# Mamba-2 mixer step: decays, readouts and Gram products issued sooner, squares summed on VectorE, softplus in fewer operations

## The reference

```
zxbcdt = x @ W_in                         # gate, xBC (x, B, C), dt
xBC = silu(depthwise_conv4(xBC))
dt = softplus(dt + dt_bias);  A = -exp(A_log);  dA = exp(dt * A)
h = h * dA[t] + (dt[t] * x[t]) outer B[t];   y[t] = h . C[t]     # scan over 1024 tokens, 16 heads
y = (y + D_skip * x) * silu(gate)
y = y * rsqrt(mean(y*y) + eps) * norm_w
out = y @ W_out
```

## Time and profile before

| | |
|---|---|
| median of 3 runs | 1135.15 us |
| the profiled execution | 1135.18 us |
| its span, first to last instruction | 1133.1 us |
| TensorE busy | 1071.9 us (95%) |
| VectorE busy | 749.0 us (66%) |
| ScalarE busy | 574.2 us (51%) |
| GpSimd busy | 319.3 us (28%) |

### The profile page before, as it was taken

How to read it: one execution, slowest core, us unless ns; L and a number is a source line. 1 busy time by engine, 2 the same in 40 slices (tenths; PEclk the granted TensorE clock), 3 DMA queues, 4 the chain that set the end, 5 groups by cost and what they waited for, 6 DMA issues and landing times.

```text
span 1133.1 us, 18155 instructions
## 1 busy us (share of the span) xinstructions
PE 1071.9 (95%) x6912; PEld 934.0 (82%) x6912; DVE 749.0 (66%) x1311; ACT 574.2 (51%) x1190; POOL 319.3 (28%) x433
## 2 busy tenths in 40 slices
PE   6889999999999997889999999899999999999997
PEld 6778888888888885788998998887888888888886
DVE  6899999999999998657766687765432133223213
ACT  6856767676767673645665556563212311321220
POOL 1012223130313214343434444313312321321331
PEclk9899999999999999989999999999999999999999
DMA  5504031322313056501011101408012002002001
GB/s 197 199 3 147 31 116 47 101 60 87 108 39 127 2 201 196 194 2 29 11 38 38 38 1 38 140 19 282 15 38 75 1 19 93 1 1 75 1 1 56
DMA packets 41590, 81.22 MB, mean 72 GB/s; under 512 B 7456, under 2 KB 13472, under 8 KB 39456
## 3 DMA queue, kind: packets, MB, share of 16 engines
q1 hardware_dynamic: 41504, 80.06, 21.2%
HBM read 67.19 MB, written 12.85 MB: 71 GB/s over the span
## 4 chain that ended last, share of the span: by engine, by line
PE 60%; DVE 24%; ACT 7%; issue 5%; POOL 2%; DMA 1%; DVEq 0%; SPq 0%; POOLq 0%; ACTq 0%
PE banks L1853 20%; PE banks L801 12%; PE banks L1866 10%; PE banks L1502 8%; DVE a_L L658 4%; DVE a_xs L575 3%; PE banks L1472 3%; PE banks L931 2%; DVE c_gx L1366 1%; DVE c_cv L1342 1%; PE banks L923 1%; DVE a_L L672 1%; ACT c_a L1243 1%; DVE a_ygl L701 1%; PE banks L881 1%
## 5 line engine op out<-in xcount | busy, mean ns | idle before, releaser
L1753 ACT ACTIVATE d_sg<-banks,d_gs 128x512 f32<-128x512 f32 x64 | 44.0, 688 | 224.8 <-PE banks L1853 224.8
L1796 DVE SCALAR_TENSOR_TENSOR d_h<-banks,d_us,d_sg 128x512 f32<-128x512 f32 x64 | 48.1, 751 | 163.6 <-PE banks L1853 151.3
L1727 POOL TENSOR_TENSOR d_hl<-d_h,d_hh 128x512 fp32r<-128x512 f32 x64 | 83.2, 1300 | 158.3 <-ACT d_hh L1757 158.2
L575 DVE SCALAR_TENSOR_TENSOR a_xs<-a_xpre,a_cvec,a_xs 128x256 f32<-128x256 f32 x192 | 100.3, 537 | 6.4 <-ACT a_xs L446 1.8
L1866 PE MATMUL banks<-d_wd,d_hh 128*128 128x512 f32 x256 | 101.1, 395 | 0.0
L1866 PE MATMUL banks<-d_wd,d_hl 128*128 128x512 f32 x256 | 100.9, 394 | 0.0
L331 POOL TENSOR_TENSOR a_sg<-a_sg 128x512 f32<-128x512 f32 x16 | 24.5, 1533 | 221.8 <-ACT a_sg L438 221.8
L658 DVE TENSOR_TENSOR_SCAN a_L<-a_L,a_ident 128x512 f32<-128x512 f32 x64 | 78.4, 1225 | 2.2
L801 PE MATMUL banks<-a_xth,a_wxh 128*128 128x256 f32 x256 | 75.7, 296 | 0.4 <-DVE a_wxl L566 0.4
L462 ACT ACTIVATE a_xdt<-banks,a_dt 128x64 f32<-128x64 f32 x256 | 56.5, 349 | 36.4 <-PE banks L881 36.4
L801 PE MATMUL banks<-a_xth,a_wgh 128*128 128x256 f32 x256 | 74.9, 293 | 0.0
(11 more groups left out here) (285 smaller groups left out, 3144.6 us busy)
## 6 DMA issues: line engine op xcount, KB each, us to landing
a_L<-decays SPq DMA_DIRECT2D x16, 1024.0 KB, 5.1
a_xf<-in_x SPq DMA_DIRECT2D x16, 256.0 KB, 2.9
a_xr<-in_x SPq DMA_DIRECT2D x16, 256.0 KB, 2.7
tokens<-a_xr SPq DMA_DIRECT2D x16, 256.0 KB, 4.0
c_xb<-tokens SPq DMA_DIRECT2D x16, 256.0 KB, 3.2
d_xin<-tokens SPq DMA_DIRECT2D x16, 256.0 KB, 5.0
d_r<-tokens SPq DMA_DIRECT2D x16, 256.0 KB, 2.7
d_wd_codes<-in_down_w SPq DMA_DIRECT2D x4, 1024.0 KB, 9.1
```

What stands on the lines that cost most here:

```text
L575: ins = dve.scalar_tensor_tensor(out=dst, in0=src[:, k:k + T], scalar=vec[:, k:k + 1], in1=dst, op0=ALU.mult, op1=ALU.add)
L1727: pool.tensor_tensor(hl[:, m, :], h32[:, m % 2, :], hh[:, m, :].bitcast(F32), ALU.subtract).then_inc(s_hl, 1)
L1753: act.activation(sg[:, m % 2, :], ps_g[:, m % 2, :], ACT.Silu, scale=gs[:, m:m + 1]).then_inc(s_sg, 1)
L1796: dve.scalar_tensor_tensor(out=h32[:, m % 2, :], in0=ps_u[:, m % 2, :], scalar=us[:, m:m + 1], in1=sg[:, m % 2, :], op0=ALU.mult, op1=ALU. ...
```

## The change

Line numbers below are those of the kernel before for the old code. Five things change:

- ScalarE does `decay` and `bc_out` ahead of `high_y(2s-1)` and `square(2s-1)`, and `gram` ahead of `evict(s, 3)`.
- TensorE does `gram` between the two channel blocks of `x_proj(s, 3)`, `turn_z` in the middle of the first channel block of `x_proj(s, 0)`, and the second `sum_sq` behind `out_proj(2s-1)`.
- The additions of squares go from GpSimd to VectorE, the first two of the three; the third is left out, and `sum_sq` takes the last two blocks in two accumulating matmuls.
- `soft` has one operation, a reciprocal and a product in its second part in place of the flag, and one operation in its third part in place of five.
- VectorE's `low(2s-1)`, `mean_sq` and the additions have new places among the `conv_m`.

```diff
@@ gpsimd
-        def tree(n):
-            pool.wait_ge(s_sq, n + 1)
-            order(pool.tensor_tensor(sq[:, 0:4], sq[:, 0:4], sq[:, 4:8], ALU.add))
-            order(pool.tensor_tensor(sq[:, 0:2], sq[:, 0:2], sq[:, 2:4], ALU.add))
-            pool.tensor_tensor(sq[:, 0], sq[:, 0], sq[:, 1], ALU.add).then_inc(s_tree, 1)
...
-                tree(C * s - 2)
-                tree(C * s - 1)
                 scale(C * s - 2)
+                norm(C * s - 2)
                 scale(C * s - 1)
-                norm(C * s - 2)
@@ scalar
             evict(s, 2)
+            decay(s)
+            bc_out(s)
             if s:
                 high_y(C * s - 1)
                 square(C * s - 1)
-            decay(s)
-            bc_out(s)
+            gram(s)
             evict(s, 3)
-            gram(s)
@@ vector
                 dve.tensor_scalar(u, e, 1.0, None, ALU.add).then_inc(s_dt, 1)
                 dve.wait_ge(s_dt, 2 * s + 2)
-                order(dve.tensor_scalar(one, u, 1.0, None, ALU.is_equal))
+                order(dve.tensor_scalar(r, u, -1.0, SMALLEST, ALU.add, ALU.max))
+                order(dve.reciprocal(r, r))
+                order(dve.tensor_tensor(r, e, r, ALU.mult))
             else:
                 dve.wait_ge(s_ln, s + 1)
-                order(dve.scalar_tensor_tensor(out=u, in0=u, scalar=-1.0, in1=one, op0=ALU.add, op1=ALU.add))
-                order(dve.reciprocal(u, u))
-                order(dve.tensor_tensor(l, l, u, ALU.mult))
-                order(dve.tensor_tensor(l, l, one, ALU.add))
-                order(dve.tensor_tensor(l, l, e, ALU.mult))
+                order(dve.scalar_tensor_tensor(out=l, in0=l, scalar=SMALLEST, in1=r, op0=ALU.max, op1=ALU.mult))
...
+        def tree(n):
+            dve.wait_ge(s_sq, n + 1)
+            order(dve.tensor_tensor(sq[:, 0:4], sq[:, 0:4], sq[:, 4:8], ALU.add))
+            dve.tensor_tensor(sq[:, 0:2], sq[:, 0:2], sq[:, 2:4], ALU.add).then_inc(s_tree, 1)
...
+        tree(C * NS - 2)
         low(C * NS - 1)
+        tree(C * NS - 1)
@@ tensor
-            pe.matmul(ps_y[:, j, 0, 0:1], sg[:, 0, cols(j)], ones, start=True, stop=True).then_inc(s_sp, 1)
+            pe.matmul(ps_y[:, j, 0, 0:1], sg[:, 0, cols(j)], ones, start=True, stop=False)
+            pe.matmul(ps_y[:, j, 0, 0:1], sg[:, 1, cols(j)], ones, start=False, stop=True).then_inc(s_sp, 1)
...
+                part(0, KD // 2)
+                if m == 0:
+                    turn_z(s)
+                last = part(KD // 2, KD)
+                if m == 2 * p and p == 3:
+                    gram(s)
```

More of the change, by code:

```diff
@@ L108, in mamba2 @@
     LIMIT = 80.0
+    SMALLEST = 2.0 ** -24
     Z0 = 64
@@ L162, in mamba2 @@
     btok = sb("a_btok", [P, C, N], F32)
-    z, e, u, l, one, dt, a = (sb("a_" + n, [P, C, H], F32) for n in ("z", "e", "u", "l", "one", "dt", "a"))
+    z, e, u, l, r, dt, a = (sb("a_" + n, [P, C, H], F32) for n in ("z", "e", "u", "l", "r", "dt", "a"))
     e16 = sb("a_e16", [H, T], F32)
@@ L325, in gpsimd @@
         pool.wait_ge(s_const, 15 + HQ)
-        def tree(n):
-            j = n % C
-            sq = sg[:, :, cols(j)]
-            pool.wait_ge(s_sq, n + 1)
-            order(pool.tensor_tensor(sq[:, 0:4], sq[:, 0:4], sq[:, 4:8], ALU.add))
-            order(pool.tensor_tensor(sq[:, 0:2], sq[:, 0:2], sq[:, 2:4], ALU.add))
-            pool.tensor_tensor(sq[:, 0], sq[:, 0], sq[:, 1], ALU.add).then_inc(s_tree, 1)
         def scale(n):
@@ L369, in gpsimd @@
         following_stage["bound"](0)
-        tree(C * NS - 2)
         following_stage["bounded_norm"](0)
-        tree(C * NS - 1)
         scale(C * NS - 2)
@@ L610, in soft @@
                 dve.tensor_tensor(a, dt, nega.unsqueeze(1).broadcast_to([P, C, H]), ALU.mult).then_inc(s_a, 1)
+        def tree(n):
+            j = n % C
+            sq = sg[:, :, cols(j)]
+            dve.wait_ge(s_sq, n + 1)
+            order(dve.tensor_tensor(sq[:, 0:4], sq[:, 0:4], sq[:, 4:8], ALU.add))
+            dve.tensor_tensor(sq[:, 0:2], sq[:, 0:2], sq[:, 2:4], ALU.add).then_inc(s_tree, 1)
         def mean_sq(n):
@@ L717, in vector @@
             conv_m(s, 0)
-            if s:
-                low(C * s - 1)
             conv_m(s, 1)
@@ L723, in vector @@
                 low_piece(NX + 1)
+            if s:
+                tree(C * s - 2)
             conv_m(s, 2)
+            if s:
+                low(C * s - 1)
             conv_m(s, 3)
@@ L731, in vector @@
                 mean_sq(C * s - 2)
+            if s:
+                tree(C * s - 1)
             conv_m(s, 5)
             if s:
-                mean_sq(C * s - 1)
                 residual(C * s - 2)
             conv_m(s, 6)
+            if s:
+                mean_sq(C * s - 1)
             conv_m(s, 7)
@@ L869, in x_proj, with part @@
             for m in (2 * p, 2 * p + 1):
-                last = three(ps_r[:, p % 2, m % 2, :], lambda i, k: wx[i][:, k, m * P:(m + 1) * P], lambda c, k: x[c][:, k, :], 0, KD, KD)
+                def part(first, until):
+                    return three(ps_r[:, p % 2, m % 2, :], lambda i, k: wx[i][:, k, m * P:(m + 1) * P], lambda c, k: x[c][:, k, :],
+                                 first, until, KD)
+                part(0, KD // 2)
[4 more added lines that the diff above has]
+                    gram(s)
             last.then_inc(s_xp, 1)
@@ L939, in tensor @@
         bc(0)
-        turn_z(0)
         x_proj(0, 0)
@@ L950, in tensor @@
             x_proj(s, 3)
-            gram(s)
             if s:
                 sum_sq(C * s - 2)
-                sum_sq(C * s - 1)
-            if s:
                 out_proj(C * s - 1, 0)
@@ L959, in tensor @@
                 out_proj(C * s - 1, 1)
+                sum_sq(C * s - 1)
             x_turn(s, 1)
@@ L974, in tensor @@
                 bc(s + 1)
-                turn_z(s + 1)
                 x_proj(s + 1, 0)
```

## The result

The changed kernel takes 1137.11 us (median of 20 runs, 1132.55 to 1139.93), the kernel before beside it 1134.49 (20 runs, 1132.73 to 1136.41). The ratio is 1.0018, with a 95% interval of 1.0010 to 1.0027: slower, by 1.1 to 3.1 us. I had said no change, 0.2 us faster. The profiled execution took 1138.53 us, its span is 1136.5, so it is 3.35 above that of before (1135.18).

A forecast was written before the change was run, and what follows sets the result against it. TensorE and VectorE, both nearly full, were taken to bound each other. From 1135.18, first stage +3.2, two low-clock stages -1.75, way out -1.6 and other stages 0 gave 1135.0 us; own range 1132.9 to 1137.3, full range 1130.0 to 1138.8.

The forecast's parts named there:

- The first stage, +3.2: First stage: the turn of x comes 3.0 to 4.4 us late, paid in full; +3.2 taken, bounds +1.5 and +4.4.
- the turn of z: First stage, TensorE: its four records, now behind six matmuls of the first projection, cost about 0.6 us on all projections behind.
- the Gram product: First stage, TensorE: runs only once the readouts are ready at 32.6, takes 1.1 us, ahead of the second channel block.
- my dearer case: First stage: the second channel block takes twice its full-clock 1.4 us, so silu starts at 38.2.
- up to 2.5 us come back behind the turn: First stage, behind the turn of x: up to 2.5 us regained if the clock has risen by then.
- The forecast by it, +4.4: First stage: by the skill's slow-clock-default rule the split block runs slow, costing 4.4 in place of 3.2; total 1136.2.
- The steady stages, 0 and -0.88: Middle stages: two VectorE waits swallow the freed time, 51.5 us again; the two of 52.38 gain 0.88 each, -1.75.
- the 0.62 of `soft`'s second part: Each stage, VectorE: the added reciprocal and product cost 0.62 us, lying where VectorE waits for `scan_out` anyway.
- The way out, -1.6: Behind the last stage: VectorE operations freed of GpSimd's additions, 0.4 of additions counted; matmuls start 1.6 us sooner, bounds 0 and 2.2.
- Relief on VectorE (1126.6): Rival: VectorE stays the bound and its freed time arrives, stages of 50.1 us, total 1126.6; chance 0.2.
- A half clock in the stages (1137.9): Rival: half-clock stretches in `out_proj` behind `gram` stay or move, 1.45 us each; 1137.9 with two; chance 0.25.
- The free first stage: Rival: first stage costs nothing, as its lower clock only moves and something else was late anyway; 1131.8; chance 0.1.

The follow-up runs named there:

- A: Changed kernel with stage 0's old order back, for the turn of z, the Gram product and evict(0, 3); 1131.30 us, 0.9968 to the kernel before.
- B: Changed kernel with only gram(0) and evict(0, 3) back in their old places in stage 0; 1132.81 us, 0.9975 to the kernel before.
- C: Changed kernel with only turn_z(0) back ahead of the first projection; 1135.19 us, 0.9999 to the kernel before.
- G: As A, with VectorE's low for the second tile one convolution block later; 1130.15 us, 0.9968 to the kernel before.
- I: As A, with ScalarE's high_y and square ahead of decay and bc_out again; 1130.14 us, 0.9961 to the kernel before.
- J: As A, with both sum_sq ahead of the second tile's out_proj and VectorE's additions directly behind its low; 1127.83 us, 0.9939 to the kernel before.
- E: Kernel before with only the shorter softplus (new `soft`), additions still on GpSimd, old orders; 1131.56 us, 0.9969 to the kernel before.

## Why the prediction was wrong

**The first stage, +3.2, was mis-sized, and it decided.** It cost 5.55, above my upper end of 4.4, and A, which takes it back, is faster than the changed kernel by 5.7 us. I had the right steps in the right order: the turn of z, the Gram product behind the readouts, the second block behind that, `evict`, silu, the turn of x. Two were priced too low.

- The Gram product had its price in full clock, 1.1, even in my upper end; it took 2.0 (32.62 to 34.62). The second block ran at clock 0.50, my dearer case, in 2.7 us (0.38 for its first matmul, then one every 0.21), and `evict(0, 3)` took its 1.5 (37.58 to 39.12). So silu began at 39.12 and not at 38.2, and the difference is that of the Gram product.
- The turn of z I had at "about 0.6, on all projections behind it"; A, B and C put it at 1.3 to 2.35. By luck it does not show in the sum: the readouts were ready at 32.57, where 32.6 was forecast, because the projections began 1.11 us sooner than before (14.18 for 15.29). From there the readouts took 18.39 us instead of 16.69.

And I let up to 2.5 us come back behind the turn, so that my +3.2 lay near the lower end of its 3.0 to 4.4; none came back, with the clock at 0.50 until 45.6. The rule that I had weighed as the other way, of the Trainium skill, TensorE: Matmul & The Clock Gate, part 1 (the slow clock is the default, and activity releases it), is borne out by the block: behind a wait of 3.76 us and the Gram product it ran wholly at 0.50. The forecast by it, +4.4, was still short by 1.15.

**The steady stages, 0 and -0.88, were right in their walk and short in size.** `soft` in 0.56, both waits on VectorE at the places and ended by the engines I named (1.00 and 0.42 for 1.1 and 1.0), no stage of 52.4. The stages came out at 51.25 and not 51.5; over six this is 1.28 us more gained than forecast. The sentence "bound now by TensorE's first 20 us and VectorE's last 30" is what G, I and J showed: the 31.81 us behind the second `sum_sq` and the gain once that `sum_sq` moved. What I had not seen is that this bound was not given by the kernel but made by the change: with both `sum_sq` ahead of `out_proj`, as before, a stage takes 50.77. I also had the 0.62 of `soft`'s second part "where VectorE waits for `scan_out` anyway". That wait was 0.18 in the kernel before (at 228.80) and is none now; the part is inside the 31.81 us. With its first stage repaired the whole change (A, 0.9968) is worth what the shorter softplus is worth alone (E, 0.9969).

**The way out, -1.6, was too much by 1.0.** I had the additions cost VectorE 0.4 and GpSimd nothing. They run beside GpSimd's first two stretched operations and shift `low` over its power operation: `low` runs until 447.96, and 0.55 later, at 448.51, the power operation ends, 1.53 for 0.70. Together the first operation of the second block comes 1.4 later behind the cut. The Trainium skill, SBUF — State Buffer, section Who interferes with whom, says that a VectorE instruction with two SBUF inputs contends with a GpSimd instruction that reads SBUF, over a shared port pair that is an exclusive lock, and that the order of issue decides which of them blocks. The rows agree from both sides: GpSimd's 1.53 here, started under a `low`, and VectorE's 1.28 for 0.19 in E, started under an addition. They do not where the two start together (the section on the hardware below). In the prediction I used such a rule only for `residual`, where there was room, and not here, where VectorE waited for the result.

**The rivals.** Relief on VectorE (1126.6) did not come, for the reason above; J shows that 0.48 us a stage of it was to be had. A half clock in the stages (1137.9) has the measured time nearly right and the reason wrong: no stage from 80.59 to 388.21 had one. The free first stage had the sign wrong. Sum over the profiled executions: +2.35 (first stage), -1.28 (six stages), +0.78 (last), +0.98 (way out), +0.7 (behind) is 3.53 on top of my -0.15, so 3.38, and 3.35 was measured. The last stage and what lies behind, 1.48 of it, vary by as much from run to run.

## What to carry to other kernels

Reorderings made for the steady state run once in a stage that has nothing before it: walk that first pass on its own, and give it its own order. A wait in front of half of a projection can cost that half again at the lower clock (here 2.7 us for 1.4). When two engines are 98 and 94% busy, look for the closed path through both (which instruction of one starts the fixed rest of the other), since a wait taken off elsewhere can come back before the next instruction on that path. Here one `sum_sq` of 0.36 us, placed 6.2 us too late, was worth 3 us together with the additions that feed it, and moving VectorE's own operations away from two visible waits of 1.00 and 0.42 gave 0.2 us a stage at most. And count from the event that an edit can move: a forecast time of day that comes true can hide two errors, as that of the readouts did.
